# Moving the folded matrices of the third pair of batches from ahead of the first shared unit's products to between its high and its low products

## The reference

```python
x = x + L0(x)   # per batch: a weighted sum of 8 masked 128x128 matrices, plus bias
x = x + L1(x)   # a base 128x128 matrix plus a weighted sum of 8 rank-16 products, plus bias
x = x + L2(x)   # shared gated MLP (128 -> 512 -> 128) plus the two best of 8 experts, gelu
x = x + L3(x)   # gated MLP (128 -> 256 -> 128) of the one best expert of the batch, silu, with biases
```

## Time and profile before

| what | value |
|---|---|
| median of 3 runs | 134.24 us (134.16 to 134.31) |
| the profiled execution's own time | 134.94 us |
| its span, first to last instruction | 133.1 us |
| TensorE matmul busy | 128.1 us, 96% of the span |
| VectorE, ScalarE, GpSimd busy | 99.2, 99.1, 75.2 us |
| granted TensorE clock | 1.0 in every fortieth of the span |

### The profile page before, as it was taken

One profiled execution on the slowest core, in us unless ns is written; L12 is line 12 of the kernel. 1 busy time (PEld: TensorE's weight loads), 2 busy tenths in 40 slices (PEclk: granted clock), 3 DMA queues, 4 the chain that ended last, 5 costly groups with the idle time before them and its releaser, 6 DMA issues.

```text
span 133.1 us, 3284 instructions
## 1 busy us (share of the span) xinstructions
PE 128.1 (96%) x930; PEld 119.5 (90%) x930; DVE 99.2 (75%) x193; ACT 99.1 (74%) x205; POOL 75.2 (57%) x89
## 2 busy tenths in 40 slices
PE   7799999999999999999999999999999999999990
PEld 5688888888888899999999999999999999999980
DVE  0499898797775867758868677677777676898791
ACT  3774699979956487777887877866767669989860
POOL 0038539979990028368497685963542644426770
PEclk9999999999999999999999999999999999999999
DMA  4999999999104955657766567656577565664224
GB/s 135 295 396 413 407 400 404 400 397 400 64 0 176 375 212 223 246 225 288 290 255 244 231 250 315 267 229 246 222 304 305 220 258 224 270 284 188 79 86 158
DMA packets 11490, 34.56 MB, mean 260 GB/s; under 512 B 1104, under 2 KB 2512, under 8 KB 11472
## 3 DMA queue, kind: packets, MB, share of 16 engines
q1 hardware_dynamic: 11184, 34.15, 65.7%
q10 hardware_dynamic: 288, 0.20, 0.5%
HBM read 12.32 MB, written 1.05 MB: 100 GB/s over the span
## 4 chain that ended last, share of the span: by engine, by line
PE 85%; DMA 3%; DVE 3%; ACT 1%; POOL 1%; issue 1%; SPq 1%; ACTq 0%; DVEq 0%; POOLq 0%
PE gate L298 29%; PE up L298 29%; PE acc L298 28%; DMA slabs<-third_in 3%; DVE x_res L978 1%; DVE h_pair L906 1%; DVE up L987 1%; POOL x_lo L762 1%; POOL x_res L788 1%; ACT h_pair L619 0%; ACTq L224 0%; ACT h_act L672 0%; DVE h_pair L1010 0%; SPq L258 0%; DVE acc L1003 0%
## 5 line engine op out<-in xcount | busy, mean ns | idle before, releaser
L756 POOL TENSOR_TENSOR dn_lo<-slabs,dn_hi 128x256 fp32r<-128x256 f32 x40 | 29.7, 743 | 38.9 <-ACT dn_hi L637 38.8
L613 ACT ACTIVATE h_act<-gate 128x512 f32<-128x512 f32 x48 | 28.9, 602 | 23.1 <-PE gate L298 21.1
L906 DVE TENSOR_TENSOR h_pair<-up,h_pair 128x512 fp32r<-128x512 f32 x55 | 37.6, 683 | 0.0
L916 DVE SCALAR_TENSOR_TENSOR up<-h_act,w_route,up 128x512 f32<-128x512 f32 x32 | 24.2, 755 | 16.9 <-PE up L298 16.7
L298 PE MATMUL gate<-x_hi,w_gu 128*128 128x256 f32 x160 | 33.9, 276 | 0.0
L298 PE MATMUL up<-x_hi,w_gu 128*128 128x256 f32 x158 | 33.4, 276 | 0.0
L619 ACT ACTIVATE h_pair<-up 128x512 fp32r<-128x512 f32 x55 | 32.8, 597 | 0.0
L298 PEld LDWEIGHTS gate<-x_hi,w_gu 128*128 128x128 f32 x160 | 27.1, 188 | 0.2
L298 PEld LDWEIGHTS up<-x_hi,w_gu 128*128 128x128 f32 x158 | 26.8, 188 | 0.0
L298 PE MATMUL acc<-h_pair,dn_hi 128*128 128x256 f32 x140 | 25.5, 276 | 0.0
L298 PE MATMUL gate<-x_lo,w_gu 128*128 128x256 f32 x80 | 22.1, 276 | 0.0
(11 more groups left out here) (126 smaller groups left out, 200.0 us busy)
## 6 DMA issues: line engine op xcount, KB each, us to landing
w_gu<-slabs SPq DMA_DIRECT2D x40, 512.0 KB, 3.1
slabs<-slabs_moe SPq DMA_DIRECT2D x8, 768.0 KB, 13.1
slabs<-slabs_l SPq DMA_DIRECT2D x4, 768.0 KB, 9.0
sh_raw<-slabs_shared SPq DMA_DIRECT2D x2, 384.0 KB, 5.8
x_res<-x_rest SPq DMA_DIRECT2D x1, 768.0 KB, 7.5
outT<-x_res SPq DMA_DIRECT2D x6, 128.0 KB, 2.0
slabs<-second_in SPq DMA_DIRECT2D x1, 320.0 KB, 3.1
slabs<-third_in SPq DMA_DIRECT2D x1, 256.0 KB, 4.6
```

The costliest lines, as they stand in the source:

```text
L613: nc.scalar.activation(h_act[:, u % 2, :], gate_ps[u % 2][:], ACT.Gelu_apprx_tanh).then_inc(act_done, 1)
L756: nc.gpsimd.tensor_tensor(dn_lo[:, q % W_SLOTS, :], slab_cols(at, DOWN_AT, 256), dn_hi[:, q % W_SLOTS, :].bitcast(F32), ALU.subtract).then ...
L906: V.tensor_tensor(h_lo[:, u % H_SLOTS, :], h_of(u), h_hi[:, u % H_SLOTS, :].bitcast(F32), ALU.subtract).then_inc(h_lo_done, 1)
L916: ins = V.scalar_tensor_tensor(h_of(u), h_act[:, k, :], weight, h_of(u), ALU.mult, ALU.mult)
```

## The change

The call `matrix(2)` stood ahead of unit 0's products. It now stands inside `first_shared_up`, behind the two high by high matmuls and ahead of the wait for `sh_lo_ready`.

```diff
@@ -417,6 +417,7 @@
                 parts = ((gate_ps[0], slice(0, P), gate_ready), (up_ps[0], slice(256, 256 + P), up_ready))
                 for out, w, _ in parts:
                     mm(out[:], sh_hi[:, w], x_hi[:, 0:PAIR], True, False)
+                matrix(2)
                 pe.wait_ge(sh_lo_ready, 1)
                 for out, w, _ in parts:
                     mm(out[:], sh_lo[:, w], x_hi[:, 0:PAIR], False, False)
@@ -488,7 +489,6 @@
 
             first_x2()
             matrix(1)
-            matrix(2)
             pe.wait_ge(sh_hi_ready, 1)
             first_shared_up()
             matrix(3)
```

## The result

| | before | after |
|---|---|---|
| median (22 runs each) | 134.39 us | 135.0 us |
| ratio, 95% interval | 1 | 1.0035 (1.0020 to 1.0051) |
| profiled execution: own time | 134.94 us | 134.87 us |
| profiled execution: span | 133.1 us | 133.1 us |

The change made the kernel slower by 0.35%, which is 0.47 us (0.27 to 0.69), against 0.32 us forecast. One disturbed execution of the changed kernel, at 263.53 us, is left out of the ratio. The median, 135.0 us, lies above the range given (134.28 to 134.78).

A forecast was written before the change was run, and what follows sets the result against it. TensorE, busy 96% of the span, was taken to bound the kernel; a stall of 0.13 + 0.08 + 0.11 = 0.32 us behind matrix(1), carried whole to the end, makes 134.24 + 0.32 = 134.56 us, range 134.28 to 134.78.

The forecast's parts named there:

- Terms 5 to 7: Unit 0's products: stall 0.32 us, matrix(2) still 0.45; x_lo's wait costs nothing; combine(2) 0.1 us late, covered.
- term 5: TensorE behind matrix(1): stall 0.13 + 0.08 + 0.11 = 0.32 us; matrix(2) then takes 0.45 us, change of kind free.
- Term 2: TensorE behind matrix(1): x_hi is ready at 11.33, 0.13 us after the array empties at 11.20.
- Term 3: From the end of VectorE's x_hi to the weight load that waited for it: 0.08 us, bounds 0.05 and 0.12.
- Term 4: From that weight load to the first high product's true start on TensorE: 0.11 us.
- Rival A: First high product's weights load while matrix(1) finishes, only the matmul waits: +0.18 to +0.25 us, 134.45 us; chance 0.17.
- B: Stall absorbed by slack in the tail, set by a ScalarE or GpSimd queue: 0 to +0.1 us, 134.3 us; chance 0.10.
- C: Late x_lo already costs the old order time at the low products, so not slower: down to 134.24 us; chance 0.06.
- D: Worse: x_hi later than traced, combine(2)'s delay or change of kind adds 0.15 to 0.4 us, 134.7 to 135.0; chance 0.05.
- E: Faster: the shift brings the tail's operations into a better phase, 0.3 us or more, 133.9 us; chance 0.04.

The follow-up runs named there:

- e4: Changed kernel with matrix(2) moved behind all six products of unit 0, right ahead of matrix(3): 4.21 us from first_x2 to x2(1), ratio 1.0042.
- e5: Changed kernel with matrix(3) moved ahead of unit 0's products, combine(2) waiting for three matrix pairs: 3.79 us from first_x2 to x2(1), ratio 1.0000.
- e2_before: The kernel before, unchanged, run and traced once more: 3.78 us from first_x2 to x2(1), ratio 0.9997.
- e7: Changed kernel with matrix(1) also moved between the high and the low products: 4.66 us from first_x2 to x2(1), ratio 1.0051.
- e1: The changed kernel once more, no edit: 4.21 us from first_x2 to x2(1), ratio 1.0007 against the kernel before.
- e9: The changed kernel a third time, no edit, beside new runs of before: 4.22 us from first_x2 to x2(1), ratio 1.0029.
- e10: The kernel before with third_in's transfer issued two transfers later: 3.79 us from first_x2 to x2(1), not timed.
- e3_half: Changed kernel with the first of matrix(2)'s two matmuls put back ahead of the high products: 3.98 us from first_x2 to x2(1), ratio 0.9985.
- e6: The kernel before with matrix(3) too ahead of unit 0's products: 3.80 us from first_x2 to x2(1), not timed.

## Why the prediction was wrong

**The mechanism was right.** The waits, the place, the weight load held by the wait, the undisturbed low products, the shift carried whole to the last matmul: each came as written. Terms 5 to 7 stand as well, but for the 0.32 us in term 5. `matrix(2)` takes 0.45 us wherever it lies, and changes of kind cost nothing (e4, e5). `combine(2)` came 0.09 us later in the change (3.04 us behind `first_x2` against 2.95 in e2_before), as said, and without effect; even 0.54 us later, in e7, it held nothing up.

**The size of the stall was too small: terms 2 and 3.** The prediction had 0.13 + 0.08 + 0.11 = 0.32 us, and the runs show 0.20 + 0.12 + 0.11 = 0.43.

- Term 2, the hole up to `x_hi`: 0.13 in the one trace there was, 0.20 in the second trace of the same kernel and in all three of the change. In the first, `matrix(1)` came 1.03 us behind `first_x2`, because `L850` ended late; in those others 0.95. `x_hi` itself was where the prediction had it, ready 1.70 or 1.71 us behind `first_x2` in all 13 traces. One execution's distance between two engines was taken as fixed, and the bounds moved only terms 3 and 4.
- Term 3, VectorE's end to the load: 10.88 to 11.00, 0.12, the upper of the two bounds. The value of the earlier trace rows was right, but the reason given for it, the wait right ahead of an fp32r product, does not hold: `x_lo`'s load also stands ahead of an fp32r product and came 0.05 behind `x_lo`'s end, 12.33 to 12.38, and again in e4 (12.31 to 12.36). The prediction counted two such places and had a third in its own rows. Why it is 0.05 us at some and 0.12 us at others stays open.
- Term 4, the load, was 0.11 as said. Rival A, by which it would be hidden, is out: the load started after the wait in every run that had one. That TensorE's queue pulls loads ahead of matmuls in flight (the Trainium skill, TensorE: Matmul & The Clock Gate, section "Architectural detail: the array is 16× 32×32, not 1× 128×128") is seen where nothing waits (11.35 ahead of 11.58 in the trace after), not across a wait.

Together: 0.32 us forecast, 0.04 more by term 3, 0.07 more by term 2, 0.43 us. Counted from `first_x2`, the changed kernel did almost what was forecast: `matrix(3)` came 3.77 us behind it (12.95 - 9.18), forecast 3.74 (13.36 - 9.62). What the prediction had wrong beyond those 0.03 us is the kernel before, which usually takes 3.78 us there and took 3.87 in the one trace at hand.

**The range failed at its base.** It rested on a median of 134.24 us from three runs that spread by 0.15 us, and kept that spread as the noise. The 22 runs of before gave 134.39 and ranged over 0.95 us, and two later sets of 35 gave 134.73 and 134.69. Of the 0.44 us by which the median missed the forecast, 0.15 is this base (134.39 - 134.24), 0.11 the stall (0.43 - 0.32), and 0.18 remains between the medians' difference of 0.61 and the stall's 0.43. That last part has no cause shown; it is within what repeated comparisons scatter (the two later differences of medians were -0.12 us in e1 and +0.31 in e9). A loss of 0.43 us on the median first shown would have been 134.67, inside the range.

**The other rivals.** B (absorbed) is refuted by the constant 115.97 to 116.00 us. C, a late `x_lo`, has no case among the traces: the load waited for `x_lo` in e2_before, e4 and e10, but the matmuls lost at most 0.02. D named the median that was measured (134.7 to 135.0) and "`x_hi` later than in the trace" as a way to it. Against `matrix(1)` it was later, but by 0.07 us, not by the 0.15 us or more that D needs, and its other two causes added nothing; that the median came out at 135.0 is owed to the base, the stall of 0.43 us and the 0.18 us without a cause shown. E is not seen.

**What stays open.** What made the first trace's stretch 3.87 us is narrowed down, not shown. There `L843` ended late (7.54, below), VectorE had no pause behind it, and the first `L850` began 1.92 us after that end and only 0.16 us ahead of `first_x2`. The trace of e3_half has a milder form of it: the same comparison ended at 6.88, `L850`'s operation began 1.91 us later at 8.79, 0.22 us ahead of `first_x2`, and `matrix(1)` came 0.97 us behind `first_x2`. In the other traces 1.96 us or more lay between the two, `L850` began 0.24 to 0.25 us ahead of `first_x2`, and `matrix(1)`, where it stood next in the list, came at 0.96 us or less. So a late `L843` goes with a smaller hole, in two traces. No run forced that.

## What to carry to other kernels

A matmul whose operands are early is worth, as filler in front of one whose operands are late, as much of the hole as it covers: here 0.43 of its 0.45 us, and the next 0.45 us nothing (e6). To price its removal, take the hole with the signal and the weight load in it (here 0.20 + 0.12 + 0.11 us), not only the distance between two ends. Where executions differ by more than the effect, measure between two marks on the bound engine around the change, and check that the rest is constant; the two spans here were equal while the changed kernel took 0.35 us longer between the marks. A single trace gives the mechanism, but a distance between two engines in it can be 0.07 us off the usual one.

## What the hardware showed unasked

**Where the spread of the times comes from.** Since the middle is constant to 0.03 us, the rest lies at the two ends. `first_x2` started between 8.63 us (e9) and 9.74 us (e2) in the timed kernels. The landing of the first transfers goes with it: `third_in` landed 3.4 us after its issue in e9 and 4.0 us in e2, and with `third_in` issued later, in e10, `first_x2` started at 10.67. Whether it accounts for all of the spread wasn't tried. At the end, issuing two output transfers takes SyncE 0.81 us in some executions and up to 2.38 us in others; in e7 one of the two alone took 1.99 us, against 0.36 us at the median of six. Its queue in e2_before, then in e7_both_behind:

```profile
129.46 0.81 SPq L290 DMA_DIRECT2D outT<-x_res  x2
130.31 0.45 SPq L292 DMA_DIRECT2D outT<-x_res  x1
```

```profile
130.02 2.38 SPq L290 DMA_DIRECT2D outT<-x_res  x2
132.44 0.43 SPq L292 DMA_DIRECT2D outT<-x_res  x1
```

In e7 the span ended 4.8 us behind the start of the last matmul (134.9 - 130.06), in e2 3.6 us (133.1 - 129.50). What delays the issue wasn't tried.

**VectorE held by GpSimd.** `L843`, a comparison of 128x64 elements with two inputs in SBUF, took 0.22 to 0.47 us. In the first trace of before it ran beside GpSimd's addition:

```profile
7.00 0.46 POOL L723 TENSOR_TENSOR slabs<-slabs 128x128 f32<-128x128 f32 x1 [2.81 <-DMA slabs<-fourth_in]
...
7.07 0.47 DVE L843 TENSOR_TENSOR hit<-rest,shift_pick 128x64 f32<-128x64 f32 x1
```

and in e10, with the addition long over, alone:

```profile
8.12 0.23 DVE L843 TENSOR_TENSOR hit<-rest,shift_pick 128x64 f32<-128x64 f32 x1
```

`L843` never ended sooner than 0.07 us behind the addition, and where it took longer than 0.23 us it ended 0.07 to 0.08 us behind it: 7.54 and 7.46 above, 6.99 and 6.92 in e1, 6.38 and 6.30 in e9. The Trainium skill (GPSIMD Engine Reference, section "Specifications") says that GpSimd's SBUF interfaces are shared with VectorE and contended by VectorE instructions with two SBUF inputs; the rows fit that. `L841`, a reduction with one input, kept its 0.22 us beside the addition in e2 (6.34, beside 6.33).
